# Adjacency layers with residual norms: the order of the first loads, of the sync queue, and two centrings folded into weights

## The chip, the cores and the metric

One core of a Trainium2 chip runs the whole program. The metric is the device time of one execution in microseconds, the median of several runs. The kernel is written by engine: TensorE (PE), VectorE (DVE), ScalarE (ACT), GpSimd (POOL) and the sync engine (SP), which issues most transfers. Each engine runs its instructions in the order written, and semaphores tie the engines together.

## The reference

There are 8 graphs of 1500 nodes with 64 features, and a sparse 0/1 adjacency matrix for each. Four layers follow one another, each `x = layernorm(x + layer(x))`:

```python
x = _layernorm(x + gnn0(x, adj, ...))                    # layer 0: 4 heads of masked attention
x = _layernorm(x + ((adj + I) @ x) / rowsum(adj + I))    # layer 1
x = _layernorm(x + adj @ (x @ weight) + bias)            # layer 2
t = adj @ x
x = _layernorm(x + where(t > 0.5, 1, 0))                 # layer 3
```

Layer 0 takes scores `(x Ws)(x Wo)^T` for each head, masks them with the adjacency, bends negative ones (slope 0.2), takes a softmax over the neighbours and weighs the head's features with it. A layernorm subtracts the row's mean over the 64 features and divides by the root of the variance.

## The kernel before

**Tiling.** A graph's 1500 nodes are 12 tiles of 125 rows (`NT`, `P`) and 3 slices of 500 rows (`NS`, `C`). The attention of a graph is 6 units (`UPG`): 2 pairs of heads times 3 slices, first the three slices of heads 0 and 1, then those of heads 2 and 3. A unit is 12 steps, a step one tile of 125 neighbours against the 500 rows of the slice for two heads. So a graph has 72 steps (`SPG`), the program 576, and one counter `q` runs over all of them on every engine; `r` is the step within its graph.

**A step.** PE fills two banks with the mask (L564) and the scores (L566), ACT bends them into a ring of 24 rows in SBUF (`LS`, L729), DVE keeps a running maximum (L868 to L874). At the unit's end PE turns the maxima (L577), DVE reduces them (L880, `row_maxima`), and SP sends them through memory to all partitions (`spread_maxima`, L366 and L372, tile `MB`). 18 steps behind the fill (`LAG`), POOL subtracts the maxima for two steps of three (L475) and DVE for the third (L888). Two steps later ACT takes the exponential (L737), then PE weighs (L603). POOL's subtractions of steps 3, 6, 9, ... also wait for DVE's last one.

**Layers 1 to 3** of graph b run between the attention steps of graph b+1. A layernorm starts at the steps `MEANS` (25, 43, 61, and 79, which is step 7 of the graph after): the mean (DVE L952), then one step later the centring (DVE L956), the square (ACT L786), the sum (DVE L961), the power on POOL (L480), the scaling (DVE L973), the split into two half-precision parts (ACT L790, POOL L484). Nine PE pieces of 12 matmuls against the turned adjacency (`collect`, L646) and three turns back with a weight or an identity (`turn_back`, L656) give the next layer, and DVE adds them to a base in `Y` (`add_up`, L988 to L993). That base is written by POOL in `prepare`, one pass over `Y` for layer 1 (L489) and one for layer 2 (L492). For the last graph the same work is done alone, by slices, at the end (L709, L718, `centred`, `summed`, `end_prepare`).

**The adjacency.** POOL casts it with its own transfers into memory as fp8 (`load`, L434, four a slice). SP then turns a slice with six transposing transfers (`turn_slice`, L351) and adds a row of ones behind them (L355), for which it waits until the six have landed. At the start POOL issues the casts of slice 0, makes constants, and issues those of slices 1 and 2 at once. SP turns slice 0, adds its ones, then sends the features.

**The features.** `load_features` (L333) sends one pair of heads: four times six transfers (L330) from `PARTS` into `FO` and `FS`. For graph b+1 heads 0 and 1 go at r = 37, heads 2 and 3 at r = 1 of its own graph. Both wait until the former user's fills are over.

**SP's order.** `spread_maxima` of the unit before stands at r = 3, 15, 27, 39, 51, 63. Slices are turned at 6, 18 and 42 (`TRANSPOSES`), features go at 1 and 37, rows of x at 11 and 29, the output at 13. SP does not follow the steps, it stops only at its waits:

```python
if turned_at(q - 1) is not None:
    spread_maxima(turned_at(q - 1))
if slice_at(q):
    turn_slice(slice_at(q))
if r == 1 and 1 <= b < B:
    load_features(b, 1)
```

Of the kernel before, what the change touches and what calls it, by code (L numbers as in the profile page):

```python
# [7 lines left out]
H, D = 4, 16  # L8
# [47 lines left out]
CONSTS = 16  # L56
LINKS = 4 * 3
# [9 lines left out]
TRANSPOSES = {6: 1, 18: 2, 42: 3}  # L67
# [8 lines left out]
NEIGHBOURS = {26: 0, 27: 1, 30: 2}  # L76
# [4 lines left out]
def adj_resnorm(nc, x, adj, wv, wself, wother, bias0, w2, bias2, out):  # L81
# [13 lines left out]
    with ctx:  # L95
# [29 lines left out]
        RDEN1 = sb("RDEN1", [P, NT], f32)  # L125
# [7 lines left out]
        WW = sb("WW", [128, 2, F], f32)  # L133
# [22 lines left out]
        fo_in = [sem(f"fo_in{i}") for i in range(PAIRS)]  # L156
        ones_in = sem("ones_in")
# [30 lines left out]
        y_ready = sem("y_ready")  # L188
# [18 lines left out]
        end_base = sem("end_base")  # L207
# [96 lines left out]
        def link_of(b, l, n):  # L304

            return LINKS * b + 3 * l + n + 1

# [14 lines left out]
        def _(sp):  # L322
# [10 lines left out]
            def load_features(b, p):  # L333
# [4 lines left out]
                for h in (2 * p, 2 * p + 1):  # L338
                    load_parts(FO[:, h, :], fo_in[p], 1, h)
                    load_parts(FS[:, h, :], fs_in[p], 0, h)  # L340

            def turn_slice(g):
# [7 lines left out]
                for q in range(NQ):  # L350
                    sp.dma_start_transpose(AT[:, slot, q:q + 1, :, :].rearrange("p q n k -> p q (n k)").bitcast(bf16),  # L351
                                           pairs[first + q * P:first + q * P + CP * (N // KK)].rearrange(
                                               "(n m) -> n m", n=CP)[:, 0:128]).then_inc(at_turned[slot], 16)
                sp.wait_ge(at_turned[slot], 16 * NQ * (g // RS + 1))
# [26 lines left out]
            load_rows(0, XA[:, :, :], xa_in)  # L381
            sp.wait_ge(ones_in, 1)
            turn_slice(0)

            sp.wait_ge(lo_ready, NS)
            for h in range(2):
                load_parts(FO[:, h, :], fo_in[0], 1, h)
            load_features(0, 1)
            for q in range(END):
# [18 lines left out]
                if r == 37 and b + 1 < B:  # L408
                    load_features(b + 1, 0)
# [4 lines left out]
            for p in range(PAIRS):  # L414
                sp.wait_ge(fs_in[p], 16 * 2 * NF * B)
                sp.wait_ge(fo_in[p], 16 * 2 * NF * B)
# [4 lines left out]
        def _(pool):  # L421
# [17 lines left out]

            pool.dma_start(cast[:, 0:PAD], adj[0:2 * NS, 0:PAD]).then_inc(pad_in, 16)  # L440
# [3 lines left out]
            const(nc.gpsimd.memset(ID[:, :], 0.0))  # L444
            diagonal(ID[:, :], 0, 128, 1.0)
# [9 lines left out]
            const(nc.gpsimd.memset(WW[:, 0, :], 0.0))  # L455
            for c in range(2):
                diagonal(WW[:, 0, :], F * c, F, 1.0)
# [28 lines left out]
            def prepare(b, l):  # L486
                if l == 0:
                    pool.wait_ge(den_seq, 3 * (b + 1))
                    nc.gpsimd.tensor_tensor(Y[:, :, :], X[:, :, :], RDEN1[:, :].unsqueeze(2).to_broadcast([P, NT, F]),  # L489
                                            ALU.mult).then_inc(y_ready, 1)  # L490
                else:
                    nc.gpsimd.tensor_tensor(Y[:, :, :], X[:, :, :], B2[:, :].unsqueeze(1).to_broadcast([P, NT, F]),  # L492
                                            ALU.add).then_inc(y_ready, 1)

            for q in range(END):
# [10 lines left out]
                at = layer_at(q, BASE)  # L506
                if at and at[1] < 2:
                    prepare(*at)

            def end_prepare(l, c):  # L510
                pool.wait_ge(end_x, 3 * l + c + 1)
                rows, cols = slice(ST * c, ST * (c + 1)), [P, ST, F]
                if l == 0:
                    factor, op = RDEN1[:, rows].unsqueeze(2).to_broadcast(cols), ALU.mult
                else:
                    factor, op = B2[:, :].unsqueeze(1).to_broadcast(cols), ALU.add
                nc.gpsimd.tensor_tensor(Y[:, rows, :], X[:, rows, :], factor, op).then_inc(end_base, 1)
# [6 lines left out]
            for l in range(4):  # L524
                for c in range(NS):
                    end_power(l, c)
                    if c and l < 2:
                        end_prepare(l, c - 1)
                if l < 2:
                    end_prepare(l, NS - 1)  # L530
# [3 lines left out]
        def _(pe):  # L534
# [15 lines left out]
            def fill_z(q):  # L550
# [89 lines left out]

            def collect(b, l, c, part):
# [3 lines left out]
                for m in range(ST * part, ST * (part + 1)):  # L645
                    last = nc.tensor.matmul(M1[:, 0:C], XP[:, m, :], AT[:P, (NS * b + c) % RS, m // KK, PAD:CP, m % KK],  # L646
                                            start=(m == 0), stop=(m == NT - 1))
# [3 lines left out]
            def turn_back(b, l, c):  # L651
                pe.wait_ge(yt_ready, 9 * b + 3 * l + c + 1)
                ring_free(place["W", b, l, c])
                z = banks("W", b, l, c)
                for k in range(ST):
                    last = nc.tensor.matmul(z[:P, 0, k * F:(k + 1) * F], YT[:, k * P:(k + 1) * P],  # L656
                                            WW[:, 1 if l == 1 else 0, :], start=True, stop=True)
# [15 lines left out]
            pe.wait_ge(ones_in, 1)  # L673
            pe.wait_ge(rest_ready, NS)
# [27 lines left out]
            for l in range(3):  # L702
                for q in range(NS):
                    pe.wait_ge(end_low, 3 * l + q + 1)
                    for c in range(NS):
                        if l and q == 0:
                            pe.wait_ge(end_taken, 3 * (l - 1) + c + 1)
                        for m in range(ST * q, ST * (q + 1)):
                            last = nc.tensor.matmul(end_banks(c)[:, 0, 0:C], XP[:, m, :], AT[:P, (NS * (B - 1) + c) % RS, m // KK, PAD:CP, m % KK],  # L709
                                                    start=(m == 0), stop=(m == NT - 1))  # L710
                        if q == NS - 1:
                            last.then_inc(end_y, 1)
                for c in range(NS):
                    if l:
                        pe.wait_ge(end_added, 3 * (l - 1) + c + 1)
                    pe.wait_ge(end_taken, 3 * l + c + 1)
                    for k in range(ST):
                        last = nc.tensor.matmul(end_banks(c)[:P, 1, k * F:(k + 1) * F], parts[c][:, k * P:(k + 1) * P],  # L718
                                                WW[:, 1 if l == 1 else 0, :], start=True, stop=True)
# [427 lines left out]
```

## Time and profile before

| what | value |
|---|---|
| median of 3 runs | 1612.44 us (1610.42 to 1614.21) |
| profiled execution, its own time | 1610.97 us |
| its span, first to last instruction | 1609.2 us |
| mean granted TensorE clock | 0.952 of full |
| busy: PE, DVE, ACT, POOL | 84%, 81%, 77%, 67% |
| first fill of PE (L564) | at 62.3 us |
| steps of graphs 1 to 7 | some 184 us a graph |

A view of the profile lists instructions in order of time (start, length, engine, line, operation, output<-input, count; in brackets how long the engine sat idle before and what released it). Others group them by line, give the busy time of each engine in a stretch, or list waits.

### The profile page before, as it was taken

Reading aid. Unit: us, or ns where it says so; the run is one execution under the profiler, and the core shown is the slowest. Engines: PE = TensorE matmul, PEld = TensorE weight load, DVE = VectorE, ACT = ScalarE, POOL = GpSimd, SP = SyncE. Lnnn points to the kernel's source line nnn. Section 1 sums busy time; section 2 is a strip of 40 time slices with the busy share of each in tenths; the row PEclk is TensorE's granted clock in tenths of the full one; section 3 lists DMA queues with packets and bytes.
Section 4 is the critical chain, followed back from the end, with each engine's and each line's share of the span. In section 5 each row is a group of like instructions: output and inputs, shape, how many; then the busy total and the mean of one; then the engine's idle time right before and its main releaser. Section 6 shows DMA issues by size and latency. Waiting matters only on the chain.

```text
span 1609.2 us, 21519 instructions
## 1 busy us (share of the span) xinstructions
PE 1352.6 (84%) x7440; PEld 664.2 (41%) x7440; DVE 1305.0 (81%) x1561; ACT 1239.9 (77%) x1427; POOL 1076.6 (67%) x571
## 2 busy tenths in 40 slices
PE   3378798898988988898989988899888889899666
PEld 2143344444444444444444444444444444344323
DVE  1368887988888888988788888988789888988775
ACT  1268888888888879888888887978798888988631
POOL 2036876778666876778667876768767886877322
PEclk9979898999999999999999999999999999999967
DMA  9625352424434244434325344333524243201000
GB/s 83 83 57 79 45 84 53 66 52 47 85 60 76 32 61 85 54 63 46 77 47 88 38 56 82 50 67 37 88 53 71 51 53 65 56 13 27 13 10 10
DMA packets 144978, 91.13 MB, mean 57 GB/s; under 512 B 102420, under 2 KB 132570, under 8 KB 144858
## 3 DMA queue, kind: packets, MB, share of 16 engines
q1 hardware_dynamic: 129766, 71.01, 21.6%
q0 software_dynamic: 13904, 18.12, 14.6%
q10 hardware_dynamic: 1200, 0.63, 0.3%
q8 instruction: 59, 0.97, 0.3%
q14 instruction: 49, 0.40, 0.1%
HBM read 103.33 MB, written 21.38 MB: 78 GB/s over the span
## 4 chain that ended last, share of the span: by engine, by line
PE 42%; DVE 25%; issue 15%; ACT 8%; POOL 6%; SPq 2%; DMA 1%; DVEq 0%; ACTq 0%; POOLq 0%
DVE RP L874 10%; PE M L603 9%; PE M L646 8%; PE Z L564 7%; PE Z L566 6%; POOL LS L475 4%; PE Z L577 4%; DVE LS L888 4%; ACT LS L729 4%; ACT LS L737 3%; PE Z L656 2%; SPq L351 2%; PE Z L612 1%; PE Z L709 1%; DVE RSTD L961 1%
## 5 line engine op out<-in xcount | busy, mean ns | idle before, releaser
L475 POOL TENSOR_TENSOR LS<-LS,MB 125x1000 f32<-125x1000 f32 x372 | 870.7, 2357 | 431.9 <-DVE LS L888 277.8
L729 ACT ACTIVATE LS<-Z 125x1000 f32<-125x1000 f32 x576 | 573.9, 998 | 145.6 <-PE Z L566 144.8
L737 ACT ACTIVATE LS<-LS 125x1000 f32<-125x1000 f32 x576 | 595.4, 1035 | 67.7 <-POOL LS L475 42.5
L874 DVE TENSOR_TENSOR RP<-LS,RP 125x1000 f32<-125x1000 f32 x480 | 575.6, 1199 | 65.4 <-ACT LS L729 44.6
L564 PE MATMUL Z<-AT,BI 126*125 126x500 fp8e4 x1152 | 364.6, 399 | 135.5 <-ACT LS L729 59.4
L603 PE MATMUL M<-LS,V 125*18 125x500 f32 x2304 | 317.5, 625 | 42.4 <-ACT LS L737 39.7
L566 PE MATMUL Z<-FS,FO 96*125 96x500 bf16 x1152 | 349.2, 385 | 0.0
L888 DVE TENSOR_TENSOR LS<-LS,MB 125x1000 f32<-125x1000 f32 x204 | 283.7, 1395 | 9.0 <-DMA MB<-row_maxima 2.5
L564 PEld LDWEIGHTS Z<-AT,BI 126*125 126x125 bf16 x1152 | 133.3, 141 | 306.8 <-ACT LS L729 130.9
L566 PEld LDWEIGHTS Z<-FS,FO 96*125 96x125 bf16 x1152 | 162.4, 141 | 92.7 <-issue 10.3
L646 PE MATMUL M<-AT,XP 125*128 125x500 fp8e4 x756 | 196.9, 384 | 0.4 <-ACTq L779 0.4
L646 PEld LDWEIGHTS M<-AT,XP 125*128 125x128 f16 x756 | 64.6, 98 | 156.4 <-issue 98.4
L603 PEld LDWEIGHTS M<-LS,V 125*18 125x18 f32 x2304 | 39.8, 97 | 166.1 <-issue 93.3
L868 DVE TENSOR_SCALAR RP<-LS 125x1000 f32<-125x1000 f32 x48 | 57.7, 1203 | 54.2 <-ACT LS L729 49.4
L577 PE MATMUL Z<-ID,RUN 125*125 125x125 f32 x384 | 93.2, 386 | 6.6 <-DVE RUN L872 3.3
L577 PEld LDWEIGHTS Z<-ID,RUN 125*125 125x125 f32 x384 | 91.6, 323 | 15.8 <-DVE RUN L872 8.5
L880 DVE TENSOR_REDUCE LMAX<-Z 125x8 f32<-125x1000 f32 x48 | 57.5, 1198 | 35.3 <-PE Z L577 34.4
L480 POOL TENSOR_TENSOR RSTD<-RSTD,NHALF 125x12 f32<-125x12 f32 x28 | 65.1, 2325 | 27.8 <-DVE RSTD L963 25.4
L656 PEld LDWEIGHTS Z<-WW,YT 128*125 128x125 f32 x504 | 63.3, 189 | 23.3 <-issue 17.6
L656 PE MATMUL Z<-WW,YT 128*125 128x64 f32 x504 | 63.9, 270 | 0.0
L777 ACT ACTIVATE YT<-M 128x500 f32<-128x500 f32 x63 | 36.8, 585 | 34.2 <-PE M L646 34.2
L612 PEld LDWEIGHTS Z<-E,O 128*125 128x125 f32 x384 | 49.7, 197 | 28.0 <-issue 22.7
(125 smaller groups left out, 919.6 us busy)
## 6 DMA issues: line engine op xcount, KB each, us to landing
MB<-row_maxima SPq DMA_DIRECT2D x48, 500.0 KB, 3.9
adj_cast<-in_adj_dram POOLq DMA_DIRECT2D x96, 183.1 KB, 4.4
FO<-PARTS SPq DMA_DIRECT2D x192, 46.9 KB, 2.1
FS<-PARTS SPq DMA_DIRECT2D x180, 46.9 KB, 2.1
XP<-in_x_dram SPq DMA_DIRECT2D x8, 336.0 KB
XA<-in_x_dram SPq DMA_DIRECT2D x8, 336.0 KB
out_dram<-X SPq DMA_DIRECT2D x7, 375.0 KB
AT<-adj_cast SPq DMA_TRANSPOSE x144, 2.8
```

Of the source, the lines that this page charges most:

```text
L475: nc.gpsimd.tensor_tensor(rows, rows, MB[:P, u % 2, :, :], ALU.subtract).then_inc(sub_pool, 1)
L564: nc.tensor.matmul(z[:P, hh, :], BI[:, :], AT[:P + 1, g % RS, pair, PAD:CP, k], start=True, stop=False)
L566: last = nc.tensor.matmul(z[:P, hh, :], FO[:, 2 * p + hh, m * P:(m + 1) * P], FS[:, 2 * p + hh, s * C:(s + 1) * C], start=False, stop=True)
L577: last = nc.tensor.transpose(z[:P, hh, c * P:(c + 1) * P], RUN[:, u % 2, hh, c:C:ST], ID[:P, :P])
L603: last = nc.tensor.matmul(M0[VW * n:VW * n + VC, 0:C], V[:, b % 2, e % STEPS, 2 * p + hh, :], LS[:P, e % RL, hh, :], start=(p == 1 and j = ...
L612: last = nc.tensor.matmul(z[:P, 0, k * 2 * VC:(k + 1) * 2 * VC], O4[:, k * P:(k + 1) * P], E[:, :, :].rearrange("p h o -> p (h o)"), start ...
L646: last = nc.tensor.matmul(M1[:, 0:C], XP[:, m, :], AT[:P, (NS * b + c) % RS, m // KK, PAD:CP, m % KK], start=(m == 0), stop=(m == NT - 1))
L656: last = nc.tensor.matmul(z[:P, 0, k * F:(k + 1) * F], YT[:, k * P:(k + 1) * P], WW[:, 1 if l == 1 else 0, :], start=True, stop=True)
L729: nc.scalar.activation(LS[:P, q % RL, :, :], banks("Z", q)[:P], ACT.Prelu, alpha=SLOPE).then_inc(bent, 1)
L737: nc.scalar.activation(rows, rows, ACT.Exp, scale=0.25).then_inc(exps, 1)
L874: nc.vector.tensor_tensor(run, rows, run, ALU.max).then_inc(maxed, 1)
L888: nc.vector.tensor_tensor(rows, rows, MB[:P, u % 2, :, :], ALU.subtract).then_inc(sub_dve, 1)
```

## The change

Four things are done.

1. **Start.** POOL makes the identity first, waits for the first rows of x and the attention weights, and then casts slice 0. The casts of slices 1 and 2 each wait until the slice before is turned. The first `FO` transfers are issued by POOL, `XA` is loaded after the features are split, and the ones of slice 0 follow its transposes directly.
2. **Sync queue.** Slices are turned at r = 3, 15 and 47, their ones added three steps later. Features go by single heads (12 transfers each): heads 2 and 3 at r = 7 and 12, heads 0 and 1 of the next graph at r = 39 and 41, so behind the maxima of r = 39. Rows of x go at r = 10.
3. **No base on POOL.** `prepare` and `end_prepare` go. Layer 1's own rows are added by PE, with four identity matmuls (`own_rows`) behind each slice's collection; layer 2's bias by PE too, with one matmul of identity times a broadcast of `B2` (`bias_rows`) ahead of the turn back. DVE's `add_up` then adds to `X`.
4. **Two centrings in the weights.** The turn back of layers 1 and 2 uses matrices whose rows are centred (`WW[:, 2]`, `WW[:, 1]`) and a centred bias, made once at the start by five DVE instructions. As `X` is centred already, the mean (L952) and the centring (L956) of these two layernorms go; layers 0 and 3 keep them.

The core of the diff:

```diff
-TRANSPOSES = {6: 1, 18: 2, 42: 3}
+TRANSPOSES = {3: 1, 15: 2, 47: 3}
+ONES_AFTER = 3
+CENTRED = (0, 3)
+MIXES = (2, 1, 0)
...
-            load_rows(0, XA[:, :, :], xa_in)
             sp.wait_ge(ones_in, 1)
             turn_slice(0)
-
+            add_ones(0)
             sp.wait_ge(lo_ready, NS)
-            for h in range(2):
-                load_parts(FO[:, h, :], fo_in[0], 1, h)
-            load_features(0, 1)
+            load_rows(0, XA[:, :, :], xa_in)
...
+                if slice_at(q - ONES_AFTER):
+                    add_ones(slice_at(q - ONES_AFTER))
-                if r == 1 and 1 <= b < B:
-                    load_features(b, 1)
-                if r == 11 and b + 1 < B:
+                if r == 7 and b < B:
+                    load_features(b, 2)
+                if r == 12 and b < B:
+                    load_features(b, 3)
+                if r == 10 and b + 1 < B:
...
-                if r == 37 and b + 1 < B:
-                    load_features(b + 1, 0)
+                if r in (39, 41) and b + 1 < B:
+                    load_features(b + 1, (r - 39) // 2)
...
+            const(nc.gpsimd.memset(ID[:, :], 0.0))
+            diagonal(ID[:, :], 0, 128, 1.0)
+            pool.wait_ge(early_in, 3 * 16)
+            pool.wait_ge(xf_in, 32)
             pool.dma_start(cast[:, 0:PAD], adj[0:2 * NS, 0:PAD]).then_inc(pad_in, 16)
...
+            pool.wait_ge(lo_ready, NS)
+            for h in range(2):
+                for n, pair in enumerate(TERMS):
+                    pool.dma_start(FO[n * D:(n + 1) * D, h, :],
+                                   PARTS[F + h * D:F + (h + 1) * D, pair[1], :]).then_inc(fo_first, 16)
             for g in range(1, NS):
+                pool.wait_ge(at_turned[g - 1], 16 * NQ)
                 for k in range(ST):
                     load(g, k)
...
-                at = layer_at(q, BASE)
-                if at and at[1] < 2:
-                    prepare(*at)
...
+            def own_rows(bank, c):
+                for k in range(ST):
+                    last = nc.tensor.matmul(bank[:, k * P:(k + 1) * P], XP[:, ST * c + k, :], ID16[:, :],
+                                            start=False, stop=(k == ST - 1))
+                return last
+            def bias_rows(bank):
+                nc.tensor.matmul(bank[:P, 0:ST * F], ID[:P, :P], B2[:, :].unsqueeze(1).to_broadcast([P, ST, F]),
+                                 start=True, stop=False)
...
             def square(b, l):
-                act.wait_ge(dve_seq, link_of(b, l, 1))
+                if l in CENTRED:
+                    act.wait_ge(dve_seq, link_of(b, l, 1))
+                else:
+                    act.wait_ge(added, 9 * b + 3 * l)
...
             def normalise(l, c):
-                centred(l, c)
+                if l in CENTRED:
+                    centred(l, c)
                 summed(l, c)
...
-                if layer_at(q, 0):
-                    mean(*layer_at(q, 0))
+                at = layer_at(q, 0)
+                if at and at[1] in CENTRED:
+                    mean(*at)
```

## Rows read from the trace of the kernel before

**Rows 1.** The page: busy time of each engine, and the chain by engine.

```profile
PE 1352.6 (84%) x7440; PEld 664.2 (41%) x7440; DVE 1305.0 (81%) x1561; ACT 1239.9 (77%) x1427; POOL 1076.6 (67%) x571
...
PE 42%; DVE 25%; issue 15%; ACT 8%; POOL 6%; SPq 2%; DMA 1%; DVEq 0%; ACTq 0%; POOLq 0%
```

**Rows 2.** Timeline of the start, 0 to 110 us.

```profile
18.59 31.24 SPq L351 DMA_TRANSPOSE AT<-adj_cast  x6
...
52.18 0.81 SPq L355 DMA_DIRECT2D AT<-ONE  x1
...
62.30 1.07 PE L564 MATMUL Z<-AT,BI 126*125 126x500 fp8e4 x2 [35.53 <-DMA FO<-PARTS]
...
75.81 8.01 SPq L351 DMA_TRANSPOSE AT<-adj_cast  x6
...
87.31 1.10 PE L564 MATMUL Z<-AT,BI 126*125 126x500 fp8e4 x2 [10.27 <-DMA AT<-ONE]
...
94.19 1.20 DVE L880 TENSOR_REDUCE LMAX<-Z 125x8 f32<-125x1000 f32 x1 [1.01 <-PE Z L577]
...
101.59 5.05 POOL L475 TENSOR_TENSOR LS<-LS,MB 125x1000 f32<-125x1000 f32 x2 [87.44 <-DMA MB<-row_maxima]
...
107.37 0.73 SPq L355 DMA_DIRECT2D AT<-ONE  x1
```

**Rows 3.** DMA issues of 0 to 70 us: count, KB each, us to landing.

```profile
adj_cast<-in_adj_dram POOLq DMA_DIRECT2D x12, 183.1 KB, 12.9
...
WA<-nn_attention_kernel_dram ACTq DMA_DIRECT2D x2, 16.0 KB, 5.2
...
WV<-in_L_gnn_kernel_dram ACTq DMA_DIRECT2D x1, 16.0 KB, 14.1
```

**Rows 4.** The chain in order of time: the first casts.

```profile
4.24 14.26 DMA adj_cast<-in_adj_dram
```

**Rows 5.** DMA issues of the whole span, same columns.

```profile
adj_cast<-in_adj_dram POOLq DMA_DIRECT2D x96, 183.1 KB, 4.4
...
AT<-adj_cast SPq DMA_TRANSPOSE x144, 2.8
```

**Rows 6.** Timeline of POOL, graph 0 and graph 5.

```profile
160.29 10.10 POOL L475 TENSOR_TENSOR LS<-LS,MB 125x1000 f32<-125x1000 f32 x4 [7.32 <-DMA MB<-row_maxima]
...
977.25 4.58 POOL L475 TENSOR_TENSOR LS<-LS,MB 125x1000 f32<-125x1000 f32 x2 [4.66 <-DMA MB<-row_maxima]
...
1044.36 1.47 POOL L489 TENSOR_TENSOR Y<-X,RDEN 125x768 f32<-125x768 f32 x1
...
1091.39 2.77 POOL L492 TENSOR_TENSOR Y<-X,B 125x768 f32<-125x768 f32 x1
```

**Rows 7.** Timeline of SP's issues at r = 39 of graph 5.

```profile
1059.05 3.75 SPq L330 DMA_DIRECT2D FS<-PARTS  x6
1062.89 1.02 SPq L366 DMA_DIRECT2D row_maxima<-LMAX  x2
```

**Rows 8.** Waits, whole span: total us, times, longest.

```profile
ACT LS L737 <- POOL LS L475: 42.5, 66, 6.5
```

**Rows 9.** Busy time in two stretches of graph 5 (layers 1 and 2): us, PE, PEld, DVE, ACT, POOL, clock.

```profile
1070.60:1098.80 28.20, 24.82 (x148) 12.12 (x148) 27.09 (x33) 25.08 (x28) 23.81 (x11) 1.00 0.14 33
1112.60:1140.70 28.10, 23.06 (x120) 10.12 (x118) 24.91 (x29) 22.62 (x26) 22.46 (x13) 0.94 0.42 47
```

**Rows 10.** Groups by line: busy us, mean ns.

```profile
L956 DVE SCALAR_TENSOR_TENSOR Y<-MEAN,Y 125x768 f32<-125x768 f32 x21 | 23.9, 1140 | 0.0
...
L952 DVE TENSOR_REDUCE MEAN<-Y 125x12 f32<-125x768 f32 x21 | 20.0, 953 | 0.7
...
L1033 DVE SCALAR_TENSOR_TENSOR Y<-MEAN,Y 125x256 f32<-125x256 f32 x9 | 4.0, 442 | 0.3
```

**Rows 11.** The chain in graph 3: a piece of collection and a turn back.

```profile
691.98 0.84 PE M L646 x4
692.83 0.82 PE Z L656 x8
```

More of the change, by code:

```diff
@@ L304, in link_of, with fo_count @@
         def link_of(b, l, n):
-            return LINKS * b + 3 * l + n + 1
+            return LINKS * b + BEFORE[l] + (n if l in CENTRED else 0) + 1
+        def fo_count(p, graphs):
+            return 16 * 2 * NF * (graphs - (p == 0))
         def by_vector(e):
@@ L454, in _ @@
                 diagonal(E[:, n % 2, :], VW * n, VC, 1.0)
-            const(nc.gpsimd.memset(WW[:, 0, :], 0.0))
-            for c in range(2):
-                diagonal(WW[:, 0, :], F * c, F, 1.0)
+            for w in (0, 2):
+                const(nc.gpsimd.memset(WW[:, w, :], 0.0))
+                for c in range(2):
+                    diagonal(WW[:, w, :], F * c, F, 1.0)
             const(nc.gpsimd.memset(DS[:, 0:VC - 1], 0.0))
             const(nc.gpsimd.memset(DS[:, VC - 1:VC], 1.0))
+            pool.wait_ge(lo_ready, NS)
[3 more added lines that the diff above has]
+                                   PARTS[F + h * D:F + (h + 1) * D, pair[1], :]).then_inc(fo_first, 16)
             for g in range(1, NS):
+                pool.wait_ge(at_turned[g - 1], 16 * NQ)
                 for k in range(ST):
@@ L505, in _ @@
                     subtract(e)
-                at = layer_at(q, BASE)
-                if at and at[1] < 2:
-                    prepare(*at)
[L510 to L517, printed above, removed]
             def end_power(l, c):
@@ L646, in collect @@
                     last = nc.tensor.matmul(M1[:, 0:C], XP[:, m, :], AT[:P, (NS * b + c) % RS, m // KK, PAD:CP, m % KK],
-                                            start=(m == 0), stop=(m == NT - 1))
+                                            start=(m == 0), stop=(m == NT - 1 and l > 0))
+                if part == 2 and l == 0:
+                    last = own_rows(M1, c)
                 if part == 2:
@@ L654, in turn_back @@
                 z = banks("W", b, l, c)
+                if l == 1:
+                    bias_rows(z[:, 0, :])
                 for k in range(ST):
                     last = nc.tensor.matmul(z[:P, 0, k * F:(k + 1) * F], YT[:, k * P:(k + 1) * P],
-                                            WW[:, 1 if l == 1 else 0, :], start=True, stop=True)
+                                            WW[:, MIXES[l], :], start=(l != 1), stop=(l != 1 or k == ST - 1))
                 last.then_inc(turned_back, 1)
@@ L709, in _ @@
                             last = nc.tensor.matmul(end_banks(c)[:, 0, 0:C], XP[:, m, :], AT[:P, (NS * (B - 1) + c) % RS, m // KK, PAD:CP, m % KK],
-                                                    start=(m == 0), stop=(m == NT - 1))
+                                                    start=(m == 0), stop=(m == NT - 1 and l > 0))
+                        if q == NS - 1 and l == 0:
+                            last = own_rows(end_banks(c)[:, 0], c)
                         if q == NS - 1:
@@ L716, in _ @@
                     pe.wait_ge(end_taken, 3 * l + c + 1)
+                    if l == 1:
+                        bias_rows(end_banks(c)[:, 1])
                     for k in range(ST):
                         last = nc.tensor.matmul(end_banks(c)[:P, 1, k * F:(k + 1) * F], parts[c][:, k * P:(k + 1) * P],
[L719 removed]
+                                                WW[:, MIXES[l], :], start=(l != 1), stop=(l != 1 or k == ST - 1))
                     last.then_inc(end_back, 1)
@@ L814, in _ @@
             act.wait_ge(const_ok, CONSTS)
+            nc.scalar.activation(ID16[:, :], ID[:P, :P], ACT.Copy).then_inc(id_ready, 1)
             for q in range(END):
@@ L937, in neighbours @@
                     return
-                dve.wait_ge(den_seq, 3 * b + n)
-                if n == 1:
-                    nc.vector.reciprocal(RDEN[:, :], DEG[:, :]).then_inc(den_seq, 1)
-                else:
-                    nc.vector.tensor_scalar(RDEN1[:, :], RDEN[:, :], 1.0, None, ALU.add).then_inc(den_seq, 1)
+                dve.wait_ge(den_seq, 2 * b + n)
+                nc.vector.reciprocal(RDEN[:, :], DEG[:, :]).then_inc(den_seq, 1)
             def rows_of(l):
@@ L1068, in _ @@
             dve.wait_ge(const_ok, CONSTS)
+            dve.wait_ge(weights_in, 4 * 16)
+            nc.vector.tensor_reduce(WSUM[:, 1:3], WW[:, 1:3, :], AX.X, ALU.add).then_inc(wc_ready, 1)
+            nc.vector.tensor_reduce(BSUM[:, :], B2[:, :], AX.X, ALU.add).then_inc(wc_ready, 1)
+            dve.wait_ge(wc_ready, 2)
+            for w in (1, 2):
+                nc.vector.scalar_tensor_tensor(out=WW[:, w, :], in0=WSUM[:, w:w + 1].to_broadcast([128, F]), scalar=-1.0 / F,
+                                               in1=WW[:, w, :], op0=ALU.mult, op1=ALU.add).then_inc(wc_ready, 1)
+            nc.vector.scalar_tensor_tensor(out=B2[:, :], in0=BSUM[:, :].to_broadcast([P, F]), scalar=-1.0 / F,
+                                           in1=B2[:, :], op0=ALU.mult, op1=ALU.add).then_inc(wc_ready, 1)
             for q in range(END):
@@ L1099, in _ @@
                 if q == LAST_ROWS:
-                    for n in range(3):
+                    for n in range(2):
                         neighbours(B - 1, n)
```

77 lines of the change are left out of this document (38 added, 39 removed).

## The prediction

> **What bounds the kernel now.** I read the page first: no engine is full. PE is busy 84% of the span, DVE 81%, ACT 77%, POOL 67%, and the chain that ends last changes hands among PE (42%), DVE (25%), ACT and POOL [rows 1]. So the time has to be read by stages, and there are four.
>
> The start. PE's first fill is at 62.3 us [rows 2]. The reader is to see why: the six transposes of slice 0 take SP from 18.59 for 31.2 us, while those of slice 1 take 8.0 us. Beside the first run eight more casts, issued before anybody needs them. Then come the ones (52.2) and, behind them on SP, the first `FO`, which PE waits for 35.5 us. Slice 1 is fit for use at 87.3 only (PE idle 10.3 us for it), its fills let the first maxima be found 8.1 us later (94.19 + 1.20 = 95.4), and POOL's first subtraction is at 101.6. The ones of slice 2 go at 107.4.
>
> Then graph 0, with no layers beside it, and the graphs 1 to 7 at some 184 us each. There I read the timeline of POOL and the issues of SP. At r = 39 the maxima go out at 1062.89, right behind `load_features`, whose last six transfers end at 1062.8: four such groups of 3.75 us, 15 us in all, stand in front of them [rows 7]. POOL's wait for the maxima is 7.3 us at that place in graph 0, and 4.7 us at r = 3 of graph 5, where the other pair of heads goes out [rows 6]. ACT, whose exponential needs the subtraction, waits 42.5 us for POOL in the whole span [rows 8]. In the stretches of the layernorms of layers 1 and 2, DVE is the fullest engine: 27.1 of 28.2 us and 24.9 of 28.1 [rows 9]. Between them, in the collections, the chain is PE without a gap: a piece of four matmuls 0.84 us, a turn back 0.82 us [rows 11]. Last comes the end, where the layers of graph 7 run alone.
>
> **The sum is made against the profiled execution**, 1611.0 us with 1609.2 of span and 1.8 around it; the median of the runs stands 1.5 us above it.
>
> **Start.** The casts of slice 0 begin later, behind the attention weights. These land 5.2 us after issue (`WA`) or 14.1 us (`WV`) [rows 3], the latter in the traffic of the casts, which is now held back; with `WV` issued at 2.3 us and the quicker figure POOL is free at 7.5. The two pads take some 1.4 us more. Four casts together took 14.3 us with everything beside them [rows 4]; one cast lands in 4.4 us over the whole run, against 12.9 in the start [rows 3, 5]. Bounds for four are thus 4.4 + 3 issues of 0.5 = 6 and 14.3; I take 10, nearer to the undisturbed row as nothing else is cast then. Slice 0 is in memory at 19, where it was before. Its transposes take 8.0 of issue and 2.8 to land [rows 2, 5], to 30, the ones 2.8 more: the first fill is at 33, not 62. By then the features are there: their split waits for `WV`, whose 14.1 us shrink, and `FO` goes by POOL's queue (12 issues), `FS` by ACT's, beside the transposes.
> Slice 1 is cast from 30 (10 us), turned (10.8) and given its ones (2.8): 54, not 87.3. The maxima are found at 62. But SP has more to do before it sends them: ones to 52, head 2 (7.5 us, two groups of 3.75 [rows 7]), a row load of 1, head 3 (7.5): 68. The maxima take 6.2 us to reach POOL (95.4 to 101.6 [rows 2]), so POOL starts at 74, 27 us earlier. Slice 2, cast from 51, is turned behind the maxima: ones land at some 84, against 109.4 (107.4 + 2.0): 25 us earlier. Features and transposes share the engines of the DMA in this stretch, so I take 24 off. Bounds: 32 when nothing disturbs, 10 when the transposes stay half as slow as the first ones.
>
> The Trainium skill, "DMA: Bandwidth & Descriptors", section "Issuing engines are not separate DMA queues", says that transfers issued by several engines interleave on the same 16 DMA engines, so that another queue saves issue time alone. The slow first transposes of the trace agree, and no row shows how much of their time the eight casts are to blame for; read strictly it makes rival 2. The same page's fit (section "Anatomy of one DMA — SWDGE (gpsimd) path", 2 us and 436 bytes a ns) would give an estimate of some 9 us for 3 MB of casts.
>
> **Graph 0.** The features of graph 1 now go behind the maxima of r = 39: POOL's wait of 7.3 us goes [rows 6], and so does a lesser one at its last unit. Below it lies DVE's own work, so I take 8 of some 10; bounds 3 and 10.
>
> **Graphs 1 to 7, gains.** At r = 3 the same wait (4.7 us) goes; POOL has a slack of some steps, and 1.3 us of it reaches ACT (bounds 0 and 4.7). At r = 39 PE is what the chain runs on, so I take nothing (bounds 0 and 2). `prepare` held POOL 1.5 and 2.8 us [rows 6] in front of subtractions that ACT waited for: 1.2 us of the first. The second lies in the stretch of layer 1's norm, where DVE loses 0.95 + 1.14 = 2.1 us [rows 10] of 27.1, and ACT's own 25.1 [rows 9] is next: I take 2.1 for both together, bounds 0 and 3.1. For layer 2, where DVE is less full, 1.5 (bounds 0 and 2.1 + 1). Sum 1.3 + 1.2 + 2.1 + 1.5 = 6.1.
> **Costs.** PE gets four identity matmuls of 125 columns behind each of layer 1's three collections. The trace has none of the kind; a quarter of the piece of 0.84 is 0.21, the whole piece is the upper bound, and I take 0.3, as 125 columns are a quarter of its 500. The bias is 256 columns of fp32 once, where a turn back does as many with four weight loads in 0.82 [rows 11]: between 0.4 and 0.82, taken 0.55. Three of each make 2.5 us a graph (2 to 5), and they lie where the chain is PE, so all of it counts.
> Net 6.1 − 2.5 = 3.6 a graph, seven times 25, less the one norm of layer 3 that graph 1 does not have: 24. Bounds: 0, if PE's work eats all, and 43, if the upper gains hold.
> **Moved steps that I cost at nothing.** Single heads at r = 7 and 12 make SP busy up to about r = 14, and those of r = 39 and 41 with the transposes and ones after them up to about r = 50. The maxima of r = 15 and 51 stand right behind. If the cover is gone, POOL waits 1 to 2 us there, half of which it has to spare. ACT's copy into `PARTS` at r = 17 waits for head 3's transfers, 2 to 3 us ahead of it. The five DVE instructions on the weights and the half-precision identity run while PE waits for slice 0.
>
> **End.** Two norms lose a pair of 0.42 + 0.44 us [rows 10] for two slices ahead of PE's start; POOL's power stands in between, so 1.3 each of 1.8. PE's identities (12 matmuls, 0.9) and one bias (0.55) are on the path there: −1, bounds −3 and +2.
>
> Sum: 24 + 8 + 24 + 1 = 57; 1611.0 − 57 = 1554.0, and 1555.5 as a median.
>
> **Rivals.**
> 1. *PE takes back what DVE and POOL give.* PE is already the fullest engine and 42% of the chain [rows 1], and every added instruction is on it; or the maxima of r = 15 and 51 become late instead of those of r = 3 and 39. For it: the collections have no gap. Against it: the gains lie in stretches where PE has 3 to 5 us to spare [rows 9]. The steady gain is then nothing, 1555.5 + 24 = 1579.5.
> 2. *The first transposes are slow by themselves*, or through the features sent beside them, not through the casts. Slice 0 then keeps most of its 31 us, and what is won is the features ahead of it, 5 us instead of 24: 1574.5. The 8.0 us of the second slice speak against it, yet that one had no cast beside it either, so the row does not tell the two apart.
> 3. *Casting in turn puts the slices in series* and is slower than before. A slice then costs 14.3 + 31.2 + 5 = 50 us each time [rows 2, 4], and slice 2 is fit for use at 9 + 150 less an overlap of 4 = 155, not 109: 46 us of stall in graph 0. With 33 won elsewhere that is 1612.4 + 13 = 1625. It decides from 44 us a slice (9 + 3 × 44 = 109 + 33); I count 24. The quick transposes of all later slices [rows 5] speak against it.
> 4. That the change does not do what it says cannot hold for the start, as the waits are in the text; for the queue it is in rival 1.
>
> **How the numbers follow.** Forecast 0.73, rival 1 0.12, rival 2 0.10, rival 3 0.05. The forecast's own range, with half of each bound, is 1530 to 1575. 8 in 10 needs the rivals 1 and 2 too, and leaves out rival 3 and the outermost bounds: 1528 to 1590. A measurement of this kernel tells 0.2%, some 3 us, from no change. Faster: the first three, 0.95, less a little for costs that add up, 0.94; same 0.02; slower 0.04.
>
> **What would show it.** Right: the first L564 near 33 us, POOL's first L475 near 74, transposes of slice 0 in 8 to 12 us; no L475 released by `MB` at r = 39; graphs at some 180 us; L489, L492 gone, L952 and L956 at 14 instead of 28; PE busy 15 to 20 us more outside the start. Wrong: transposes of slice 0 over 20 us (rivals 2, 3), graphs still at 184 with more PE on the chain (rival 1), or POOL waiting for `MB` at r = 15 or 51.

## The result: 10 us, not 57

The changed kernel takes 1602.64 us (median of 4 runs, 1599.19 to 1603.09) against 1612.61 (4 runs) for the kernel before: a ratio of 0.9935, 95% interval 0.9916 to 0.9953. The profiled execution has a span of 1600.5 us, against 1609.2. The forecast was 1555.5 with a range of 1528 to 1590, and the time lies above both.

The spans are split at the first bend of each graph (ACT's first L729 of before, L753 of after):

| stretch | before | after | difference | forecast |
|---|---|---|---|---|
| start to the first bend | 64.3 | 36.5 | −27.8 | −24 |
| graph 0 | 158.8 | 162.1 | +3.3 | −8 |
| graphs 1 to 6, sum | 1104.1 | 1118.8 | +14.7 | −20.4 (24 − 3.6) |
| graph 7 and the end | 282.0 | 283.0 | +1.0 | −4.6 (3.6 + 1) |
| span | 1609.2 | 1600.5 | −8.7 | −57 |

So the start gave what it should, and everything behind it lost two thirds of that again. One profiled execution scatters in graph 0: it takes 162.1 us here, 163.0 in e4 and 157.7 in e9 below, which run the same instructions up to the end of graph 1. The +3.3 says that the forecast gain did not come, not that graph 0 became slower.

### The start came as forecast

The timeline of the start, after; these lines answer to [rows 2]:

```profile
16.55 8.02 ACTq L835 DMA_DIRECT2D FS<-PARTS  x12
17.15 5.76 POOL L482 DMA_DIRECT2D FO<-PARTS  x12 [1.77 <-DVE PARTS L956]
21.11 7.78 SPq L362 DMA_TRANSPOSE AT<-adj_cast  x6
...
34.53 1.06 PE L566 MATMUL Z<-AT,BI 126*125 126x500 fp8e4 x2 [16.43 <-DMA AT<-ONE]
...
55.90 1.09 PE L566 MATMUL Z<-AT,BI 126*125 126x500 fp8e4 x2 [7.04 <-DMA AT<-ONE]
...
62.44 3.70 SPq L341 DMA_DIRECT2D FO<-PARTS  x6
62.63 1.20 DVE L909 TENSOR_REDUCE LMAX<-Z 125x8 f32<-125x1000 f32 x1 [1.01 <-PE Z L579]
66.19 3.76 SPq L341 DMA_DIRECT2D FS<-PARTS  x6
69.99 1.06 SPq L380 DMA_DIRECT2D row_maxima<-LMAX  x2
...
76.38 4.58 POOL L499 TENSOR_TENSOR LS<-LS,MB 125x1000 f32<-125x1000 f32 x2 [21.35 <-DMA MB<-row_maxima]
```

The transposes of slice 0 take 7.8 us, not 31.2, although 24 feature transfers were issued beside them, from 16.55 to 24.57. PE's first fill is at 34.5 (forecast 33), slice 1 is fit for use at 55.9 (54), POOL starts at 76.4 (74). The maxima are there at 62.63 + 1.20 = 63.8, and SP sends them 6.2 us later, since it is still sending head 3; the forecast had counted that (62 and 68).

### From r = 18 on it is lost again

The mean of three steps together, graphs 1 to 6, puts the loss in one place. It is r = 18 to 23, where POOL and DVE subtract the maxima that are sent at r = 15: 6.49 + 7.22 us before, 8.47 + 9.55 after, +4.3 a graph. All other groups together are 1.9 us a graph shorter. By graph, r = 18 to 23 take 13.7 us everywhere before, and 15.2, 21.0, 14.0, 17.7, 17.4 and 22.8 after. SP's timeline of graph 6 from r = 3 to 15, after:

```profile
1135.50 0.78 SPq L380 DMA_DIRECT2D row_maxima<-LMAX  x2
1137.27 0.34 SPq L386 DMA_DIRECT2D MB<-row_maxima  x1
1137.70 9.09 SPq L362 DMA_TRANSPOSE AT<-adj_cast  x6
1148.30 0.74 SPq L369 DMA_DIRECT2D AT<-ONE  x1
1149.15 3.73 SPq L341 DMA_DIRECT2D FO<-PARTS  x6
1152.92 3.75 SPq L341 DMA_DIRECT2D FS<-PARTS  x6
1156.71 1.19 SPq L337 DMA_DIRECT2D XP<-in_x_dram  x2
1158.00 3.73 SPq L341 DMA_DIRECT2D FO<-PARTS  x6
1161.77 4.53 SPq L341 DMA_DIRECT2D FS<-PARTS  x6
1166.35 0.47 SPq L419 DMA_DIRECT2D out_dram<-X  x1
1166.92 3.27 SPq L380 DMA_DIRECT2D row_maxima<-LMAX  x2
1173.13 0.34 SPq L386 DMA_DIRECT2D MB<-row_maxima  x1
```

The same place before; output and maxima:

```profile
1175.47 0.28 SPq L404 DMA_DIRECT2D out_dram<-X  x1
1181.64 0.78 SPq L366 DMA_DIRECT2D row_maxima<-LMAX  x2
1183.66 0.34 SPq L372 DMA_DIRECT2D MB<-row_maxima  x1
```

And what hangs on it, after, on DVE, POOL and ACT:

```profile
1162.89 1.19 DVE L909 TENSOR_REDUCE LMAX<-Z 125x8 f32<-125x1000 f32 x1
...
1177.03 10.09 POOL L499 TENSOR_TENSOR LS<-LS,MB 125x1000 f32<-125x1000 f32 x4 [7.17 <-DMA MB<-row_maxima]
...
1180.36 1.04 ACT L761 ACTIVATE LS<-LS 125x1000 f32<-125x1000 f32 x1 [4.06 <-POOL LS L499]
```

From 1149 to 1170 SP issues without a gap, so that only its own order holds the maxima back. There are two delays. The maxima are found at 1164.1 and sent at 1166.9, 2.8 us late (0.4 to 2.8 in graphs 2 to 6). And from sending them to fetching them back (L380 to L386) it takes 6.2 us, against 2.0 before (1181.64 to 1183.66). Before, the 375 KB of the output had gone out 6.2 us ahead of the maxima, because SP was idle there; after, they go 0.6 us ahead. POOL waits 7.2 us, then ACT 4.1.

Neither delay costs much by itself. In graph 3 the maxima are found at 605.3 and sent 0.4 us late, behind the same output:

```profile
605.14 0.47 SPq L419 DMA_DIRECT2D out_dram<-X  x1
605.71 3.28 SPq L380 DMA_DIRECT2D row_maxima<-LMAX  x2
611.82 0.35 SPq L386 DMA_DIRECT2D MB<-row_maxima  x1
...
615.70 5.06 POOL L499 TENSOR_TENSOR LS<-LS,MB 125x1000 f32<-125x1000 f32 x2 [4.59 <-DMA MB<-row_maxima]
...
618.07 1.04 ACT L761 ACTIVATE LS<-LS 125x1000 f32<-125x1000 f32 x1 [0.18 <-POOL LS L499]
```

They are back after 6.1 us, as in graph 6, but ACT waits 0.2 us only, and the six steps take 14.0 us. In graph 1, which has no output at r = 13, the maxima go 5.6 us late behind the heads, are back after 2.3 us, and the steps take 15.2. The heads' lateness and the output's way add up against one slack of POOL: the sum is 6.5 us in graph 3 and 9.0 in graph 6.

In graph 0 the maxima are late at r = 15 (6.2 us) and at r = 51 (5.2 us), there for heads and a slice's transposes alone. Its unit 3 is 8.4 us shorter than before (23.5 against 31.9, as forecast from [rows 6]), its unit 4 is 8.8 longer (32.5 against 23.7).

The page, after, beside [rows 1]: PE has 30 us more and DVE 45 us less, POOL 30 less, and the chain has moved from DVE to PE. The prediction wanted 15 to 20 us more on PE as a sign that it was right, but these 30 are no measure of the added work: e8 below has the same number of PE's instructions and is busy 1351.1 us, at a mean granted clock of 0.952; here the clock is 0.941. Nothing in these sums tells of the loss.

```profile
PE 1383.0 (86%) x7584; PEld 682.5 (43%) x7584; DVE 1260.2 (79%) x1518; ACT 1240.8 (78%) x1428; POOL 1046.4 (65%) x566
...
PE 49%; DVE 15%; issue 12%; ACT 10%; POOL 7%; SPq 3%; DMA 3%; ACTq 0%; DVEq 0%; POOLq 0%
```

### The profile page after: what moved, and what is told of

It reads as the page before. It is cut to its first block, busy times and chain, and to the rows that moved or that the text cites. A ratio compares the mean times of both kernels' runs of the same rounds, so it can differ in the third digit from the quotient of the medians.

```text
span 1600.5 us, 21762 instructions
## 1 busy us (share of the span) xinstructions
PE 1383.0 (86%) x7584; PEld 682.5 (43%) x7584; DVE 1260.2 (79%) x1518; ACT 1240.8 (78%) x1428; POOL 1046.4 (65%) x566
## 3 DMA queue, kind: packets, MB, share of 16 engines
q1 hardware_dynamic: 129382, 70.44, 20.4%
## 4 chain that ended last, share of the span: by engine, by line
PE 49%; DVE 15%; issue 12%; ACT 10%; POOL 7%; SPq 3%; DMA 3%; ACTq 0%; DVEq 0%; POOLq 0%
PE M L660 10%; PE M L605 9%; PE Z L566 8%; PE Z L568 7%; POOL LS L499 5%; ACT LS L753 5%; PE Z L579 5%; DVE RP L903 5%; ACT LS L761 3%; PE Z L674 3%; DVE LS L917 2%; PE Z L614 2%; SPq L341 1%; DMA adj_cast<-in_adj_dram 1%; DVE X L999 1%
## 5 line engine op out<-in xcount | busy, mean ns | idle before, releaser
L753 ACT ACTIVATE LS<-Z 125x1000 f32<-125x1000 f32 x576 | 575.4, 999 | 139.4 <-PE Z L568 138.1
L566 PE MATMUL Z<-AT,BI 126*125 126x500 fp8e4 x1152 | 370.4, 404 | 99.3 <-ACT LS L753 61.4
L568 PE MATMUL Z<-FS,FO 96*125 96x500 bf16 x1152 | 355.4, 390 | 0.0
L917 DVE TENSOR_TENSOR LS<-LS,MB 125x1000 f32<-125x1000 f32 x204 | 279.7, 1376 | 8.8 <-DMA MB<-row_maxima 2.4
L449 POOL DMA_DIRECT2D adj_cast<-in_adj_dram x96 | 53.5, 559 | 27.9 <-DMA AT<-adj_cast 27.9
L674 PEld LDWEIGHTS Z<-WW,YT 128*125 128x125 f32 x504 | 63.8, 189 | 16.6 <-issue 11.6
```

The lines of the kernel that those rows point to most:

```text
L566: nc.tensor.matmul(z[:P, hh, :], BI[:, :], AT[:P + 1, g % RS, pair, PAD:CP, k], start=True, stop=False)
L568: last = nc.tensor.matmul(z[:P, hh, :], FO[:, 2 * p + hh, m * P:(m + 1) * P], FS[:, 2 * p + hh, s * C:(s + 1) * C], start=False, stop=True)
L753: nc.scalar.activation(LS[:P, q % RL, :, :], banks("Z", q)[:P], ACT.Prelu, alpha=SLOPE).then_inc(bent, 1)
L917: nc.vector.tensor_tensor(rows, rows, MB[:P, u % 2, :, :], ALU.subtract).then_inc(sub_dve, 1)
```

## The experiments

The theory: SP's new order (part 2) makes the maxima of r = 15, and in graph 0 of r = 51, late, and the rest is worth roughly what it should be. The rivals: PE takes back what DVE and POOL give (rival 1's first half), or the parts are each worth little.

### One part at a time

**e1_start_only**: the kernel before with part 1. Heads 2 and 3 of graph 0 go at r = 7.

```diff
-                if r == 1 and 1 <= b < B:
+                if (r == 1 and 1 <= b < B) or q == 7:
                     load_features(b, 1)
```

> The kernel before with part 1 of the change alone (order of the start; features by pairs as before). Theory A (the start wins 28 us and keeps it; what is lost is lost by the sync queue at r = 15): 1583 to 1588 us. Theory B (PE's added work eats the gain): the same, 1583 to 1588. Theory C (an earlier start is lost again in graph 0 whatever follows): 1600 or more.

**e2_queue_only**: the kernel before with part 2 (`TRANSPOSES`, `ONES_AFTER`, single heads, rows at r = 10).

> The kernel before with part 2 alone (features by single heads, slices turned at 3, 15, 47, ones three steps later, rows at 10). Theory A (heads, rows and output fill SP from r = 3 to 15, the maxima of r = 15 go late): 10 to 25 us slower than before, 1622 to 1637, graphs of 186 to 188 us. Theory B: the waits at r = 3 and 39 go, 5 to 15 us faster. Theory C: within 3 us of before.

**e3_weights_only**: the kernel before with parts 3 and 4.

> The kernel before with parts 3 and 4 alone (no base on POOL, own rows and bias on PE, two centrings in the weights). Theory A (the stretches of layers 1 and 2 are paced by ACT and PE, DVE and POOL only fill them): within 5 us of before. Theory B (PE's added 2.5 us a graph count in full): 8 to 18 us slower. My prediction's step (DVE and POOL set the pace there): 12 to 25 us faster.

**e5_after_old_queue**: the changed kernel without part 2, its queue as in e1.

> The changed kernel with the old sync queue (features by pairs at 1 and 37, slices at 6, 18, 42, ones behind the transposes), so parts 1, 3 and 4 without 2. If the parts add: 1613 - 13 - 5 = 1595 us, 4 to 12 us faster than the changed kernel. If the new order of the queue is needed for the others' gain: 1605 or more.

| kernel | median us (runs) | before | ratio | 95% interval |
|---|---|---|---|---|
| e1, part 1 | 1599.81 (4) | 1613.21 | 0.9906 | 0.9874 to 0.9938 |
| e2, part 2 | 1629.37 (5) | 1613.21 | 1.0091 | 1.0061 to 1.0121 |
| e3, parts 3 and 4 | 1608.23 (10) | 1613.21 | 0.9941 | 0.9911 to 0.9971 |
| e5, parts 1, 3 and 4 | 1587.12 (4) | 1610.78 | 0.9849 | 0.9818 to 0.9879 |

Part 2 by itself makes the kernel 16 us slower, and on top of the others about as much (1602.6 against 1587.1). In e2 the steps r = 18 to 23 take 8.20 + 9.36 us and the way of the maxima 6.1 to 6.8 us; in e1, e3 and e5 these steps stand at 6.49 + 7.22, as before. That settles which part the loss comes from. The single parts sum to −13.4 + 16.2 − 5.0 = −2, while −10 was measured. Parts 1, 3 and 4 together are worth 24, their single sum is 18: they add only roughly, and e5 gains more than the 4 to 12 us over the changed kernel that were expected.

e1 shows something else. Its first bend is at 37.7, 26.6 us earlier, yet the time falls by 13 alone: graph 0 takes 168.3 us in place of 158.8, with maxima sent 3 to 7 us late behind features and transposes in three of its units. The 1583 to 1588 expected of the queue theory were missed, and the time is that of theory C; e8 shows that its "whatever follows" does not hold. What makes e1's graph 0 longer was not separated.

### One number: the output behind the maxima

**e4_out_behind**: the changed kernel with the output of a graph sent at r = 17.

```diff
-                if r == 13 and b >= 2:
+                if r == 17 and b >= 2:
```

> The changed kernel with the output's transfer put behind the maxima of r = 15 (r = 17 instead of 13). Theory A: the two small transfers of the maxima no longer queue behind the 375 KB of the output; from issue to MB's issue 2 to 4 us instead of 6.1, 10 to 20 us faster than the changed kernel, 1583 to 1593. Theory B and C: 1600 to 1604.

1575.59 us (4 runs), ratio 0.976 [0.9731, 0.9789]: 27 us under the changed kernel from one number, more than the 10 to 20 expected. SP and POOL in e4, the same place of graph 6:

```profile
1143.28 4.41 SPq L341 DMA_DIRECT2D FS<-PARTS  x6
1147.79 1.01 SPq L380 DMA_DIRECT2D row_maxima<-LMAX  x2
1150.20 0.34 SPq L386 DMA_DIRECT2D MB<-row_maxima  x1
...
1158.35 0.48 SPq L419 DMA_DIRECT2D out_dram<-X  x1
```

```profile
1154.13 4.59 POOL L499 TENSOR_TENSOR LS<-LS,MB 125x1000 f32<-125x1000 f32 x2 [3.33 <-DMA MB<-row_maxima]
```

The maxima are still sent 2.8 us late here, behind head 3, but they are back after 2.4 us, and r = 18 to 23 take 6.62 + 7.43 us. Without the output's delay, the heads' lateness of 1.0 to 2.8 us costs nothing in graphs 2 to 5, 0.5 us in graph 6, and in graph 1, where it is 5.7, 1.6: POOL has most of it to spare, as the prediction said. The output in front of the maxima makes the sum too long.

### Its bytes, or one more issue?

**e9_small_output**: the changed kernel, output at r = 13, but one tile of twelve stored.

```diff
-                    sp.dma_start(out_v[b - 2], X[:, :, :].rearrange("p (q k) f -> p q k f", k=KK)).then_inc(stored, 16)
+                    sp.dma_start(out_v[b - 2][:, 0:1, 0:1], X[:, 0:KK, :].rearrange("p (q k) f -> p q k f", k=KK)[:, :, 0:1]).then_inc(stored, 16)
```

> The changed kernel with the output of a graph still at r = 13, but only one of its twelve tiles stored (32 KB in place of 375 KB). It leaves out the other eleven tiles of the outputs of graphs 0 to 6. The same number of SP's instructions stands ahead of the maxima of r = 15. If the mere number of issues ahead of them makes the maxima late, the steps r = 18 to 23 of graphs 2 to 7 stay at 8.5 + 9.6 us, the way from the write of the maxima to their return stays at 6.1 us, and the time at 1600. If it is the output's bytes, that way falls to 2.0 us while the write itself goes out 2 to 2.8 us late as before, the steps r = 18 to 23 come down to 6.6 + 7.4, and the time to 1575 to 1580.

1571.16 us (4 runs), ratio 0.9739 [0.9718, 0.976], close to e4; graphs 1 to 6 take 1090.6 us, against 1091.0 in e4. SP's timeline, graph 6:

```profile
1141.41 0.47 SPq L419 DMA_DIRECT2D out_dram<-X  x1
1141.98 0.80 SPq L380 DMA_DIRECT2D row_maxima<-LMAX  x2
1144.34 0.35 SPq L386 DMA_DIRECT2D MB<-row_maxima  x1
```

The same instructions in the same order, the maxima still 1.3 to 3.2 us late, and the way is 1.8 to 2.4 us. So it is the size of the store and not the issue: with 375 KB in front of them on SP's queue, the maxima's 4 KB come 4 us later, and the two issues themselves take 3.27 us in place of 0.80. The bytes and the packets shrink together (750 packets of 512 bytes, 125 of 256), so e9 does not tell which of them counts. The DMA rate in the changed kernel, 1166 to 1178 us in 40 slices of 0.3 us, shows them:

```profile
GB/s 30 120 40 120 47 84 77 85 94 82 72 87 92 84 110 104 113 108 69 27 1 0 0 0 0 0 0 80 213 360 333 347 154 275 246 138 259 163 62 200
```

Some 90 GB/s up to 1171.7, with the end of head 3 at its front (375 KB at 90 GB/s are 4.2 us), then nothing until `MB` is fetched: the maxima, issued from 1166.92 on, are through only when the output is. The Trainium skill, "DMA: Bandwidth & Descriptors", section "Queues, rings and completion order", says that each DMA engine takes the descriptors of a ring in order; this pair of runs agrees (6.2 us behind 375 KB, 2.4 behind 32).

That the shared queue alone does it is not shown, as no run sends the output at that time from another engine's queue. The maxima of r = 27 go out with nothing else issued by SP in the 6 us before them, but 0.9 us behind a cast that POOL issued on its own queue, here in graph 5:

```profile
1007.45 0.60 POOL L449 DMA_DIRECT2D adj_cast<-in_adj_dram  x1
1008.35 0.81 SPq L380 DMA_DIRECT2D row_maxima<-LMAX  x2
...
1012.55 0.34 SPq L386 DMA_DIRECT2D MB<-row_maxima  x1
```

They are back after 4.2 us here and after 3.0 to 4.5 in graphs 1 to 6, against 1.7 to 2.3 at r = 39, where no cast is beside them. So another queue's traffic seems to lengthen the way too, and moving the output to another queue might not have done what moving it behind the maxima did.

### The weights, and PE's part in them

**e6_centring_only**: the kernel before with part 4 alone; POOL writes the bases as before, PE gets nothing (the diff is against e3).

```diff
+            def prepare(b, l):
...
-                if part == 2 and l == 0:
-                    last = own_rows(M1, c)
...
-                if l == 1:
-                    bias_rows(z[:, 0, :])
```

> The kernel before with the two centrings in the weights alone: DVE loses 2.1 us twice a graph, POOL keeps the base, PE gets nothing. Theory A (r = 42 to 47 are paced by ACT, DVE only fills them): graphs of 182.5 to 184.5 us, 3 to 8 us faster in all, from the end (2.6 us) and from POOL's waits. My prediction's step (DVE sets the pace in the norms): 15 to 28 us faster.

**e7_base_only**: the kernel before with part 3 alone: e3, but DVE still does the mean and the centring of all four layers.

```diff
-CENTRED = (0, 3)
+CENTRED = (0, 1, 2, 3)
```

> The kernel before with own rows and bias on PE and without the base on POOL, all means and centrings kept. Theory A: PE's added work costs 1.0 to 1.8 us a graph in the collections (r = 39 to 41 and 54 to 62) and the POOL passes give 1.0 to 1.8 back (r = 36 to 38, 48, 63 to 68): within 5 us of before. Theory B: 8 to 18 us slower. Prediction's step: the POOL passes alone 1.2 to 2 us a graph against 2.5: 4 to 9 us slower.

e6 takes 1599.60 us (6 runs), ratio 0.9916 [0.9889, 0.9943]; e7 1612.14 (10 runs), ratio 1.0006 [0.9984, 1.0027]. So part 4 by itself is a gain of about 11 us and part 3 by itself none; e3, with both, gained 5. The 11 lie between the 3 to 8 of the one expectation and the 15 to 28 of the other. In e6's trace 7.1 us come from graphs 1 to 6 and the end, 3.0 from the start and graph 0, whose steps the edit does not touch. Group by group e7 gives 0.63 us a graph at r = 36 to 38 (9.75 to 9.12, `prepare` of layer 1 gone; e1, e2, e6 and e10, which keep it, have 9.58) and takes 0.9 at r = 39 and 54 to 62, where PE's additions lie: 8.88 to 9.10, 7.33 to 7.50, 8.01 to 8.44, 7.60 to 7.68. It also has 1.1 us more at r = 42 to 53; that is not explained. PE's instructions by line and form, after:

```profile
L652 PE MATMUL Z<-B,ID 125*125 125x256 f32 x46 | 14.4, 396 | 0.0
L646 PE MATMUL M<-ID,XP 125*128 125x125 f16 x84 | 8.0, 218 | 0.0
```

The identities are 8.0 / 21 = 0.38 us busy for each of 21 collections (forecast 0.3), the bias 14.4 / 23 = 0.63 for each of 23 slices (forecast 0.55). The prices were near, but of 3 a graph only 0.9 lengthens the steps.

The gain forecast at layer 1's norm did not come. There ACT, bend and exponential in turn, paces the steps. Busy time in r = 42 to 47 of graph 5 (columns: us, PE, PEld, DVE, ACT, POOL, clock, DMA share, GB/s), before and then after:

```profile
1069.60:1082.30 12.70, 10.74 (x72) 4.95 (x72) 11.46 (x18) 12.29 (x15) 9.46 (x5) 1.00 0.19 41
```

```profile
1050.30:1063.10 12.80, 10.76 (x73) 4.93 (x72) 9.88 (x18) 12.35 (x16) 9.02 (x5) 1.00 0.40 79
```

DVE falls by 1.6 us and the stretch stays: 5.78 + 6.99 us for the two groups of steps, to the hundredth the same before, after and in e6 (of all traces only e7 has more, 5.83 + 7.27). ACT is busy 12.3 of 12.7 us. The first stretch of [rows 9] covered 28.2 us, almost from this stage's start. DVE is the fullest engine only from 1082.3 on (15.6 of 16.5 us); the sum hid it.

### Graph 0 mended too

**e8_graph0_too**: e4, and in graph 0 head 2 goes before the first step and head 3 at r = 7; in all graphs the third slice is turned at r = 51, behind the maxima.

```diff
-TRANSPOSES = {3: 1, 15: 2, 47: 3}
+TRANSPOSES = {3: 1, 15: 2, 51: 3}
...
             load_rows(0, XA[:, :, :], xa_in)
+            load_features(0, 2)
...
                 if r == 7 and b < B:
-                    load_features(b, 2)
-                if r == 12 and b < B:
+                    load_features(b, 2 if b else 3)
+                if r == 12 and 1 <= b < B:
...
-                if r == 13 and b >= 2:
+                if r == 17 and b >= 2:
```

> The changed kernel with the output behind the maxima of r = 15 (as in the run before), the next graph's slice 0 turned at r = 51 instead of 47, and in graph 0 head 2 sent before the loop and head 3 at r = 7. Theory A: the maxima of units 0 and 3 of graph 0 go out at once instead of 5.6 and 5.1 us late; 8 to 15 us faster than that run, 1560 to 1568. If the start's gain is lost again whatever the queue does: 1573 to 1577.

1557.64 us (4 runs), ratio 0.9672 [0.9644, 0.9699]. The maxima of r = 51 of graph 0, first after, then e8:

```profile
139.07 7.79 SPq L362 DMA_TRANSPOSE AT<-adj_cast  x6
...
149.23 0.84 SPq L380 DMA_DIRECT2D row_maxima<-LMAX  x2
...
157.06 3.31 POOL L499 TENSOR_TENSOR LS<-LS,MB 125x1000 f32<-125x1000 f32 x1 [6.72 <-DMA MB<-row_maxima]
```

```profile
144.58 0.79 SPq L380 DMA_DIRECT2D row_maxima<-LMAX  x2
146.56 0.34 SPq L386 DMA_DIRECT2D MB<-row_maxima  x1
146.95 7.74 SPq L362 DMA_TRANSPOSE AT<-adj_cast  x6
```

Every unit's maxima in graph 0 now go out when they are found. Graph 0 takes 151.3 us (162.1 after, 163.0 in e4), unit 4 of it 23.8 (32.5 after). That is the maxima of r = 51; those of r = 15 give nothing back that can be seen, as units 0 and 1 together take 50.5 us (50.9 after). Of the 16.5 us of span under e4, graph 0 has 11.7; graph 7 and the end have 4.5, which were not traced to a cause. ACT's wait for POOL in the whole span, after and in e8, against 42.5 in [rows 8]:

```profile
ACT LS L761 <- POOL LS L499: 46.5, 52, 6.4
```

```profile
ACT LS L762 <- POOL LS L500: 24.8, 44, 1.1
```

**e10_no_pe_work**: e8 with POOL's bases kept and without PE's identities and bias (the edit of e6 on e8).

> Kernel e8 with the bases on POOL as before and without PE's identity and bias matmuls: start, queue (with graph 0 and the output mended) and the two centrings in the weights. If PE's additions and the lost bases cancel, as the run of that part by itself had it, the time is that of e8, 1555 to 1560. If centring without PE's additions keeps the 9 us that it was ahead of both together by itself (1599.6 against 1608.2), 1548 to 1552. If POOL's bases are dearer now that the maxima no longer hold POOL up, 1562 or more.

1557.47 us (5 runs), ratio 0.9649 [0.963, 0.9669]. Level with e8, as the first of the three expectations had it: PE has 1.4 us less in the whole span (1349.7 against 1351.1), the chain falls from 46% to 39% PE, POOL's busy time rises from 1042 to 1082 us, and the time is the same. The 9 us by which e6's median lay under e3's (6, each against the kernel before beside it) are not kept. Why e3 gains less than e6, when part 3 costs nothing by itself or in e8, stays open: their two intervals overlap, and e3's ten runs reach from 1593 to 1611 us, so it may be scatter.

## Why the prediction failed

**The step that failed** is "moved steps that I cost at nothing". It counted SP's heads in front of the maxima of r = 15 and 51 and priced the lateness at 1 to 2 us, half of which POOL could spare. For the heads alone that was right: 0.3 us a graph in e4. It left out the output at r = 13, which the change doesn't touch: before, it went out 6 us ahead of the maxima; with SP full it went directly ahead, and its 4 us came on top of the heads' lateness. The cost is 4.3 us a graph (r = 18 to 23), and e4's 27 us over the run. No part of the diff names that line; SP's queue from r = 3 to r = 15 written out in full, with sizes, would have. In graph 0 the lateness at r = 51 is 5.2 us, not 1 to 2; in e8, without it, unit 4 is 8.7 us shorter. That gave back the 8.4 us of the maxima of r = 39. Unit 3 of graph 0 takes 23.5 us and a unit of graphs 1 to 6 some 31, which may be why SP is not done in time there; no run tested it. At r = 15 of graph 0 the 6 us were counted in the start, and they cost nothing more.

**Rival 1** said that the maxima of r = 15 and 51 become late in place of those of r = 3 and 39; that half of it came true. Its price, a steady gain of nothing (1579.5), was too low by 23 us. Of its other half, e7 and e10 show that PE takes back what POOL gives and no more; that it takes back all is refuted by e5, which is 13 us under e1 (9 by the two ratios).

**Start**, −24: right (−25.2 at POOL's first subtraction, −27.8 at the first bend), and so were its steps, to within 3 us each. Rival 2 is refuted by the 7.8 us of slice 0's transposes with 24 feature transfers issued beside them; they had been slow beside the eight early casts, and that these were to blame is argued from the two starts, not tested by itself. Rival 3 is refuted: slice 1's fills begin 21.4 us after slice 0's, not 50. The Trainium skill, "DMA: Bandwidth & Descriptors", section "Issuing engines are not separate DMA queues", on which rival 2 leaned, has it that a second issuing engine saves issue time alone; here it did no harm either.

**Graph 0**, −8: it did not come (+3.3), and did once the queue was mended (−7.5 in e8, −5.0 in e10), as near as single traces tell.

**Graphs 1 to 7**, −3.6 a graph: −2.3 in e8 (graphs 1 to 6 −14.0 in all), made up as follows.

| term | forecast | measured, e8 against before |
|---|---|---|
| maxima of r = 3 | 1.3 | 1.4 (r = 6 to 14; e2 has 1.7, e3 none) |
| `prepare` of layer 1 | 1.2 | 0.6 (r = 36 to 38) |
| layer 1's norm | 2.1 | 0.6 (r = 48 to 53, but 0.0 to 0.3 there in e3, e4, e6, e9, e10 and after; nothing at r = 42 to 47) |
| layer 2's norm | 1.5 | 0.9 (r = 63 to 68) |
| PE's additions | −2.5 | −0.9 (r = 39 to 41, 54 to 62) |

The rest, 0.3 us a graph, is lost in groups of less than 0.2 each. Both sides were too large, gains 6.1 for 3.5 and costs 2.5 for 0.9, so the net came out near by luck. The largest gain was taken from a stretch's fullest engine, which was not the one that paced its first half, where the work was taken out; the costs were added in full, though PE had gaps beside them.

**End**, −1 with graph 7's 3.6: +1.0 after, −3.9 in e8.

With the output and graph 0's order mended, the change gives 53 us (1610.8 less 1557.6) of the 57 forecast, and the time is 2 us from the forecast. That nearness is in part luck: the start gives 3 us more than forecast, graphs 1 to 6 give 6 less, and the kernel before ran 2 us faster beside e8. The forecast described a queue that the diff did not write.

**The forecast's own range**, 1530 to 1575, does not come out of its bounds: half of each distance gives some 1540 to 1578. The upper bound of 43 for graphs 1 to 7 is seven times the 6.1 with no cost at all, not the upper gains. The time lies above either range.

## What to carry to other kernels

When a change moves transfers along a queue, write that queue out in full between two deadlines, with the bytes of each entry and the untouched entries too: a small transfer that others wait for must not stand directly behind a large store. Delays of one transfer add up against one slack, so price them together. An idle stretch of an issuing engine is cover for what stands in it, and filling it has a price at the next deadline. A gain read from an engine's busy share holds only if that engine is the one without gaps in every stage of the stretch, so cut the stretch where the pace changes.

## What was not expected of the hardware

- Behind a store of 375 KB on the same queue, two writes of 4 KB together take 3.27 us to issue instead of 0.8, and 6.2 us until their completion is seen, instead of 2.0 to 2.4. Beside one cast of 183 KB on POOL's queue it is 3.0 to 4.5 us.
- The transposes of a slice take 7.8 us beside 24 small feature transfers of two other issuing engines, and took 31.2 with eight casts of 183 KB under way.
- ACT, in a stretch in which it is busy 12.3 of 12.7 us, holds the steps to the hundredth of a us (5.78 and 6.99) while DVE's load beside it falls by 1.6 us.
